# Maxima of attention scores: masked edges two to a bank, twelve differences a pass, the keys' difference made two passes ahead

## What is computed

```
xn = _layernorm(x, axis=-1)
scores = jnp.einsum('bhqd,bhkd->bhqk', q, k) * scale
causal = jnp.tril(jnp.ones((t, t), dtype=bool))
scores = jnp.where(causal[None, None], scores, -jnp.inf)
att = jax.nn.softmax(scores, axis=-1)
y = jnp.einsum('bhqk,bhkd->bhqd', att, v)
x = x + _L0_attn_ref(xn, ...) + _L0_ffn_ref(xn, ...)
```

## Time and profile before

| | us |
|---|---|
| median of 3 runs | 1961.71 |
| lowest and highest | 1958.18, 1965.72 |
| the profiled execution | 1960.21 |
| its span, first to last instruction | 1958.4 |

### The profile page before, as it was taken

The page is one execution under the profiler, slowest core; times in us unless marked ns, Lnnn a source line. Parts: engine busy times, 40 slices in busy tenths (PEclk is TensorE's granted clock), DMA queues, the critical chain, the costliest instruction groups (busy, mean ns, idle before and its releaser), DMA issues.

```text
span 1958.4 us, 42217 instructions
## 1 busy us (share of the span) xinstructions
PE 1867.4 (95%) x13879; PEld 698.8 (36%) x13879; DVE 1695.4 (87%) x4770; ACT 1592.3 (81%) x1916; POOL 539.4 (28%) x648
## 2 busy tenths in 40 slices
PE   6899999999789999999999999999999999999998
PEld 6555565556322222222232222223222222322223
DVE  5699999999889998989999898999899999989861
ACT  2467666765269999999999899999899999989994
POOL 0122111211313423242342324144232414324220
PEclk8899999999769999999999999999999999999999
DMA  4133323334522304032341414234141413414012
GB/s 173 31 93 102 103 79 93 100 107 100 112 63 40 65 22 62 22 62 39 61 69 39 65 40 84 35 64 65 42 62 41 86 31 68 60 45 65 29 39 78
DMA packets 160327, 129.04 MB, mean 66 GB/s; under 512 B 95344, under 2 KB 144752, under 8 KB 159768
## 3 DMA queue, kind: packets, MB, share of 16 engines
q1 hardware_dynamic: 160152, 126.88, 30.0%
HBM read 74.60 MB, written 42.98 MB: 60 GB/s over the span
## 4 chain that ended last, share of the span: by engine, by line
PE 45%; ACT 14%; issue 6%; SPq 3%; DMA 3%; DVE 2%; POOL 1%; ACTq 0%; DVEq 0%; POOLq 0%
PE pv L1562 20%; ACT prob L1344 12%; PE sm L1524 10%; PE st L1547 9%; PE sm L1495 3%; PE st L1534 2%; DMA scratch_i<-inverse 2%; ACT excess L1337 1%; SPq L947 1%; DVE sm L1413 1%; ACT Y L1327 1%; SPq L1095 1%; DMA Yc<-Y 1%; PE sm L1519 0%; SPq L1106 0%
## 5 line engine op out<-in xcount | busy, mean ns | idle before, releaser
L1344 ACT ACTIVATE prob<-st 128x1024 f32<-128x1024 f32 x1088 | 1057.8, 1026 | 78.3 <-PE st L1547 70.6
L1562 PE MATMUL pv<-prob,V 128*32 128x512 f32 (+3 forms) x5120 | 596.8, 548 | 1.0 <-POOL prob L1304 0.9
L1524 PE MATMUL sm<-K,Q 48*128 48x512 f16 (+3 forms) x2112 | 560.9, 352 | 21.1 <-DVE pm L1430 4.4
L1413 DVE CUSTOM_DVE_ANT_0 sm<-sm,mask 128x128 f32<-128x128 f32 (+3 forms) x1024 | 493.3, 509 | 81.8 <-PE sm L1524 73.2
L1547 PE MATMUL st<-Q,K 50*128 50x512 f16 (+3 forms) x2560 | 479.2, 354 | 16.5 <-ACT prob L1344 12.5
L1304 POOL TENSOR_SCALAR_AFFINE_SELECT prob<-prob 128x256 f32<-128x256 f32 (+1 forms) x448 | 191.5, 442 | 939.0 <-ACT prob L1344 929.9
L1430 DVE TENSOR_REDUCE pm<-sm 128x1 f32<-128x512 f32 x640 | 414.1, 684 | 17.4 <-PE sm L1524 15.1
L1524 PEld LDWEIGHTS sm<-K,Q 48*128 48x128 f16 x2112 | 164.9, 94 | 435.2 <-DVE pm L1430 120.5
L1425 DVE CUSTOM_DVE_ANT_0 sm<-sm,excess 128x512 f32<-128x512 f32 x448 | 306.0, 718 | 15.4 <-PE sm L1524 7.6
L1337 ACT ACTIVATE excess<-st 128x1024 f32<-128x1024 f32 x220 | 224.1, 1027 | 31.4 <-PE st L1534 24.9
L1547 PEld LDWEIGHTS st<-Q,K 50*128 50x128 f16 x2560 | 123.8, 94 | 249.7 <-ACT prob L1344 163.4
(11 more groups left out here) (169 smaller groups left out, 1940.0 us busy)
## 6 DMA issues: line engine op xcount, KB each, us to landing
Q<-scratch_q SPq DMA_DIRECT2D x102, 128.0 KB, 4.4
K<-scratch_k SPq DMA_DIRECT2D x102, 128.0 KB, 7.1
x<-in_x SPq DMA_DIRECT2D x16, 512.0 KB, 4.4
scratch_v<-Rt SPq DMA_DIRECT2D x64, 128.0 KB, 2.0
scratch_r<-Rt SPq DMA_DIRECT2D x16, 512.0 KB, 3.2
V_raw<-scratch_v SPq DMA_DIRECT2D x16, 512.0 KB, 9.4
Yc<-Y SPq DMA_DIRECT2D x124, 64.0 KB
spread<-scratch_i SPq DMA_DIRECT2D x124, 64.0 KB, 2.2
```

What stands on the lines that cost most here:

```text
L1344: act.activation(prob_of(quad, k)[:, :, :], st[number % ST][:, :, :], ACT.Exp).then_inc(exp_done, 1)
L1413: i = dve.tensor_tensor_reduce(x, x, mask[:, CH - block_width(t, k):], 1.0, -3e38, ALU.add, ALU.max, best(h, t, k))
L1524: i = pe.matmul(dst[:, at:at + width], lhsT=Q[slot][r, h // 2, t * P:(t + 1) * P], rhs=K[slot][r, h // 2, k * CH:k * CH + width], start=Tr ...
L1562: i = pe.matmul(pv[2 * DH * h:2 * DH * (h + 1), CH - width:CH], lhsT=V[quad % VSLOTS][:, j, h, :], rhs=prob_of(quad, u)[:, h % 2, at:at + ...
```

## The change

Four things are edited. `maxima_sequence` collects the masked edges of four query tiles and puts them out at the second, third and fourth tile of a chunk: at the second the 256-wide edges of both pairs of heads share a bank, at the third the 128-wide edge of the first tile shares one with the 384-wide edge of the third, and the 512-wide edges at the fourth stay alone. The edges of the first tile thus come later in the sequence. `by_difference` drops the second pair of heads at odd t of c == 2. `DK` of quad + 2 is made in the pass of a quad, at the first step of c == 3, behind `place_v`; the second quad's is made ahead of the passes; SP loads KC between K and V. And `TIMETABLE`, `AHEAD` and `PROJECT_AT` are new. A pass then has 119 entries (40 edge banks with 64 blocks, 48 plain, 24 paired, 4 projections, 3 rows) and 12 differences, where it had 139 (64 edge, 40 plain, 28 paired, 4, 3) and 14. The code that reduces an edge bank already loops over its blocks.

```diff
-PROJECT_AT = (76, 91, 105, 119)
+PROJECT_AT = (64, 77, 87, 99)
...
-    return c == 3 or c == 2 and (hp == 0 or t % 2 == 1)
+    return c == 3 or c == 2 and hp == 0
...
-            c = t // SUB
+            c, place = divmod(t, SUB)
             for hp in range(G // 2):
                 pair = by_difference(c, hp, t)
                 for k in range(c):
...
                     blocks += [(role, ((2 * hp + g, t, k, 0),)) for g in range(2)]
-                blocks += [("edge", ((2 * hp + g, t, c, 0),)) for g in range(2)]
+            pairs = range(G // 2)
+            if place == 1:
+                blocks += [("edge", tuple((2 * hp + g, t, c, hp * 2 * P) for hp in pairs)) for g in range(2)]
+            elif place == 2:
+                blocks += [("edge", ((2 * hp + g, t - 2, c, 0), (2 * hp + g, t, c, P))) for hp in pairs for g in range(2)]
+            elif place == 3:
+                blocks += [("edge", ((2 * hp + g, t, c, 0),)) for hp in pairs for g in range(2)]
...
-AHEAD = 70
+AHEAD = 58
...
 TIMETABLE = (
-    "mwxmmsmwsmmxmmxmmsmmswmxmsmwmxmmswsmmwsmsmmmsmmmmssmwmmsmsmxmmwxmmsm"
-    "msmmswxmmsmwmmsmswmsmwmssmmwmmxmsmwxmmmswmmssmwmsmmswmsmmsmswmxmmxmm"
-    "msmmmsmsmwsmmmswmsmsmwsmmmswmsmmsmwmsmsmmwmsmsmmwmsmmsmwsmsmmwsmsmmw"
-    "xmmmswsmmswmmswsmmsmwmsmmsmwxmmsmwmsmmsmwmsmsmmwmsmms"
+    "mwmxmmswxmmsmmsmwmsmsmwmmsmswsmmxwmxmmsmmmsmswsmmmswsmsmmmsmmxmxmwxm"
+    "msmsmwxmmsmwsmmsmmmssmwmxmwmssmmwsmmmswsmmsmwsmmswmsmmxwsmsmmsmwsmms"
+    "mwsmsmmwxmmsmwmssmmwmsmwsmsmmwmmsmswmsmsmwsmsmmwsmmsmwsmmswmsmsmwmsm"
+    "mswmsmmswmsmmswmsmmswmsmxmwmsms"
 )
...
                     load_qk(sp, scr, (quad + 2) % NQ, Q[nxt], K[nxt], qk_loaded[nxt])
+                    if quad + 2 < NQ:
+                        load_kc(quad + 2)
                     sp.wait_ge(v_placed, quad + 1)
                     load_v(quad + 1)
...
                     load_m(quad + 1, (slot + 1) % SLOTS, 0)
-                if quad + 2 < NQ:
-                    load_kc(quad + 2)
...
                 base = 5 * quad
+                if quad:
+                    pool.wait_ge(differed, quad)
...
-                    if n == STEP_AT[2] and not last:
-                        turn, nxt = quad // SLOTS, (slot + 1) % SLOTS
-                        difference_of_keys(quad + 1, nxt, (turn + (2 if nxt == 0 else 1)) * (16 * LOADS))
                     if n == STEP_AT[TC - 1] and not last:
                         place_v(quad + 1, (slot + 1) % SLOTS)
+                    if n == STEP_AT[TC - 1] and quad + 2 < NQ:
+                        difference_of_keys(quad + 2, (quad + 2) % SLOTS, ((quad + 2) // SLOTS + 1) * (16 * LOADS))
...
             place_v(0, 0)
+            difference_of_keys(1, 1, 16 * LOADS)
             quads(body)
```

## The result

The changed kernel takes 1940.69 us, the median of 12 executions (1925.78 to 1951.82), against 1961.27 us for the kernel before (12 executions, 1954.55 to 1969.63). The ratio is 0.989, with a 95% interval from 0.986 to 0.991. I had forecast 1951 us, 10.4 less than before; it moved by 20.6. The direction and the range held, the size didn't. Whatever the kernel, a rare execution takes far longer than the others (2162.14, 2863.14 and 3436.54 us in three of the series); medians here are of the rest.

What follows compares the result with a forecast made beforehand. ACT, closely followed by DVE, was taken to bound the pass, with handovers through PE. Fifteen passes at -0.9 (-13.5), last pass -1.9, start +5: -10.4, so 1951 us against 1961.71; range 1927 to 1984.

Steps and rivals of the forecast that it cites:

- The count +2.4: DVE's work per pass: four paired banks go, eight plain ones come, +2.4 us, from 78.1 to 80.5.
- So merging takes nothing from DVE's work: Masked edges on DVE: reductions and widths stay, only 24 handovers a pass go, so sharing banks saves 0 us of work.
- DVE's idle time: Per pass: of 6.8 us idle the 3.5 of edge waits vanish, 3.3 stay, plus 0.2 for late rows.
- 1.9 to 3.3 of delay against 2.8: I take 0, bounds 0 and 0.9: KC loads delay `sums` by 2.8 us on SP, but DVE reaches its reciprocal 1.9 to 3.3 later: no cost per pass.
- The start: GpSimd makes the second quad's difference before all first masks, so c == 0 is evacuated some 5 us later, bounds +2 and +9.
- so I compare with the undisturbed one: Base pass: 84.88 us, not the next at clock 0.96 with 88.11; its -0.9 is applied to 15 passes, -13.5.
- the clock as a rival: PE less busy in each pass, so eight more passes lose 3.2 us to a lower clock: 1977 us, chance 0.06.
- The pass stays: Rival: DVE's added 2.4 us eat the gains of ACT and edges, pass 85.0, +0.1: 1966 us, chance 0.21.
- the scores wait for rows: Rival: PE stops at c == 3's first scores 0.3 to 0.9 us every pass, pass 85.9: 1983 us, chance 0.15.
- my mark of 5: Sign of a wrong forecast: `sums` or `Q<-ml` among the waits with over 5 us in total.
- DVE is fed without gaps: Rival: with all banks wide, DVE's waits on PE vanish, pass 82.4, -2.5: 1927 us, chance 0.18.
- Projections only move in the list: PE's ordered list: projections stay four a pass and only change place; PE's changes were costed at nothing.

## Why the prediction was right or wrong

**ACT: right.** 78.5 forecast, 78.8 measured.

**DVE's work: wrong by 1.3 us a pass.** The count +2.4 was right for what it counted; DVE was to go to 80.5 and went to 79.2. The step that failed is "So merging takes nothing from DVE's work". The edges' busy time fell by 20.3 us, 1.27 a pass. Where two edges follow each other with the next bank ready, they start 0.25 us apart (128 columns), and a record lasts 0.33: each overlaps the next. Where a bank was late, as mostly before, the record stands alone at its full length. I had taken the pace of the good chain as the price of all edges, both before and after. The saving shows in every kernel with the new sequence of edges (472.2 to 475.9), with shared banks or single ones, and in none with the old sequence (492.7 to 493.8). So it is the grouping and not the sharing; that it is the overlap of records is what the paces suggest, not something that a run isolated.

**DVE's idle time: 3.5 forecast, 4.1 measured** in the pass of 83.23, where the edge waits are 1.1 us in five places. I had let them vanish. The waits of the plain maxima took their place in part (17.4 us to 31.5 over the program).

**SP's queue: wrong, and the largest step that failed.** It is "1.9 to 3.3 of delay against 2.8: I take 0, bounds 0 and 0.9", for moving the keys' load in front of V's. The changed kernel waits 13.1 us for sums in eight passes in one profile and 5.5 in six in the other; in the first no pass with such a wait is under 84.1 us. Moving the load away gives 12 to 14 us (1926.98 against 1938.66, 1940.69 and, in the same series, 1940.39), nearly 1 us a pass. Both sides of the comparison were off. The delay is 1.6 us: where nothing holds it, the reciprocal stands 40.40 us after the evacuation (1209.01 in the pass that begins at 1168.61), and it stood at 38.84 before (1032.58 in the one from 993.74). The issues take 2.75 us at best, and up to 4.84. And I had one pass for a margin that varies: from K's issue to that of the sums it is 19.3 to 22.2 us in the passes before and 20.8 to 25.7 with the keys' load between them. The waits are also more than idle time of DVE: PE stands behind them, and behind the long ones the clock falls. This error makes the kernel longer, so it hid part of what the forecast missed on the other side. In the old order, where the point of use isn't later, the same move costs 37 us: 23.6 of waits on DVE, and PE, ACT and the low clock behind it.

**The pass: nearly right, by two errors that cancel.** 84.0 forecast; the fourteen passes at a mean clock of 1.00 average 83.92 (1174.92 / 14), against 84.8 for a pass before at full clock. That the number came out is luck. The shortest passes, where no reciprocal waits, are 83.22: 1.3 less by DVE's work and 0.6 more by its idle time than I had. The late sums and smaller waits put 0.7 back on average.

**The start: right in kind, near in size.** The first mask was forecast near 572 and came at 569.89, PE's first sum 572.8 and came at 570.81, the evacuation 579 and came at 577.75 (at 581.13 in the other profile). By the end of the first pass the lag was 1.0 us in one profile and 4.4 in the other (657.70 against 653.28); I had +5, with bounds of 2 and 9.

**The last pass:** -1.9 forecast, -0.6 measured (89.66 for 90.22); what follows it was 1.7 us shorter, which I had not counted. Together -2.3.

**Where the other 10 us are.** With passes at full clock on both sides the sum is 14 x (83.92 - 84.8) = -12.3, +1.0 to +4.4 at the start and -2.3 at the end: -10.2 to -13.6, against -10.4 forecast. The median says -20.6. The step that failed here is "so I compare with the undisturbed one": it puts the -0.9 of an undisturbed pass on all fifteen, and so takes the clock's low stretches as equal in both kernels. They aren't. Before, fourteen passes took 1204.54 us, 17 more than 14 x 84.8, and all 17 lie in the seven passes with a low stretch. Of the changed kernel, one profile has 14.9 us more than the other, by the late sums, and the other has next to no such time. Over all executions of both, the mean granted clock is 0.966 before (63 of them) and 0.973 after (18). Within the kernel before, 0.01 more of it goes with 11 us less (7 to 15 in the five series one by one), so the difference of 0.007 is worth some 8 us, which with the sum above makes -18 to -22. The 8 us are an estimate from how the two go together; no run changed the clock by itself. I had the clock as a rival on the slower side alone, "so I give it little"; it came on the other side.

Why it stays up more is open, but the profiles show where it falls. Before, no low stretch follows a stop of PE of 1 us or more. The last six of the seven begin 39 to 41 us behind the evacuation of c == 3, where PE's list is thin in every pass, with a low stretch or without. In the new order that place is full (9 us of a pass before, then the same distance into a pass of the changed kernel):

```profile
1026.74:1035.74 9.00, 8.32 (x61) 2.32 (x55) 8.13 (x34) 8.69 (x11) 0.78 (x2) 1.00 0.15 24
...
1201.61:1210.61 9.00, 8.95 (x74) 2.54 (x70) 8.73 (x38) 8.56 (x10) 0.41 (x1) 1.00 0.26 55
```

PE's 8.32 became 8.95, and in the changed kernel the clock falls at this place only where the sums were late. That the fuller place is the reason is argued, not shown. The kernel in which PE stood still longest, at the late keys' difference, has the lowest mean clock, 0.938.

**Rivals.** *The pass stays* and *the scores wait for rows* didn't come true: `Q<-ml` waits are 7.7 us, over my mark of 5, but they grew to 14.8 us in the kernel with the load at the end, which is shorter. *DVE is fed without gaps* (82.4) is nearer with the load moved: 83.2 us a pass, and 1926.98 us where it had 1927. The fed kernel was there to be had; the late sums kept the change from it. Both signs that I had named as wrong came: DVE busy below 79.5, and sums waiting over 5 us.

**What the sum couldn't see.** I priced the parts one by one and added them up. Alone in the old order they cost 37, 77 and 32 us, together at the old places 114, and with the new order they give 21. The additive sum came near only because both orders fit their own parts. "Projections only move in the list", and the places of the banks beside them, were the largest term of the change, 131 us between 2072 and 1941, and stood in my sum at nothing. The 131 us are against one rule for the old places, that of the last block; another rule, the place of the first block for one, wasn't tried.

## What to carry to other kernels

Where one engine feeds several from a list in a fixed order, a part of a change has no price of its own: time the parts in their order, and expect that adding or removing one without laying the list out anew can cost more than it saves. Here it cost 32 to 114 us, and the whole change saved 21. Before a group of DMA issues is moved on a queue, look for the load behind it with the smallest distance between landing and use, over many passes and not in one; six issues of 2.8 us together cost 1.9% in the old order, and moved to where the queue was idle they cost nothing. And read the price of an instruction both in a chain and alone: edges that stood among other work kept DVE busy for 4% more than the pace of a chain says.

## What the runs showed of the hardware

- A second wait on a value already reached, between two DVE operations, showed no cost: 0.988 with 24 more of them a pass, 0.989 without.
- Masked edges of equal count and width keep DVE busy 473 us when they stand in chains and 493 us when they stand between others, 4%.
- A load that lands late costs more than its wait. In the four passes of the changed kernel in which DVE waited 1.72 to 2.75 us for the sums, PE stood 1.81 to 2.84 us behind it. The granted clock was then low for 4 to 7.5 us (0.51 from 1124 to 1131 us). These passes took 14.7 us more than the same four in another execution (fourteen passes in 1189.78 and in 1174.92 us), of which the waits are 7.0. It isn't so every time: in the kernel with the second wait, waits of 2.13 and 1.86 us have no low stretch behind them, two of 2.93 and 2.95 have.
- The clock also fell without a stop of PE: before the change, seven times in fifteen passes, at places where PE had stood for less than 1 us. The mean clock was 0.973 in the changed kernel, 0.966 before, and 0.938 where PE waited 8 us in every pass.
- Six issues of the keys' load took 2.77 us on an idle queue, 2.75 to 4.84 us between K's and V's, where they stand behind twelve other issues.
